# Last recurrence of a two-layer block: the bonus on GpSimd, the first state columns on ScalarE

## The reference

```python
def step(s, rkvw):                      # h = 32 heads, i and j = 16 channels of a head
    r_t, k_t, v_t, w_t = rkvw
    a = k_t[..., :, None] * v_t[..., None, :]
    out = jnp.einsum('bhi,bhij->bhj', r_t, u * a + s)
    s = a + w_t[..., :, None] * s
    return (s, out)
_, out = jax.lax.scan(step, s0, rkvw)   # over the 112 tokens
```

## Time and profile before

| | |
|---|---|
| Median of 3 runs | 1780.87 us (1780.46 to 1786.08) |
| Profiled execution, its own time | 1791.03 us |
| Span of that execution | 1789.2 us |
| TensorE busy, share of the span | 1697.5 us, 95% |
| VectorE busy | 1167.6 us, 65% |
| ScalarE busy | 657.2 us, 37% |
| GpSimd busy | 281.2 us, 16% |
| Mean granted TensorE clock | 0.97 |

### The profile page before, as it was taken

How to read it: one execution, slowest core, us unless ns; L and a number is a source line. 1 busy time by engine, 2 the same in 40 slices (tenths; PEclk the granted TensorE clock), 3 DMA queues, 4 the chain that set the end, 5 groups by cost and what they waited for, 6 DMA issues and landing times.

```text
span 1789.2 us, 18450 instructions
## 1 busy us (share of the span) xinstructions
PE 1697.5 (95%) x6792; PEld 860.0 (48%) x6792; DVE 1167.6 (65%) x1620; ACT 657.2 (37%) x1507; POOL 281.2 (16%) x377
## 2 busy tenths in 40 slices
PE   6999999899999999999999999999989999999968
PEld 3555544345555444445555444455544445444423
DVE  1233200336999895548997965389989767999841
ACT  2466420124666222236663213256532135313111
POOL 1100000122121001121220002211200023136020
PEclk9999999889999999989999999999999999999989
DMA  7001012124111123351120232520022415232131
GB/s 254 12 29 52 1 52 90 50 83 141 37 45 54 41 93 127 97 159 37 37 62 22 88 114 89 157 78 9 16 76 78 135 52 159 85 118 74 56 101 44
DMA packets 75143, 138.82 MB, mean 78 GB/s; under 512 B 16624, under 2 KB 26736, under 8 KB 75056
## 3 DMA queue, kind: packets, MB, share of 16 engines
q1 hardware_dynamic: 60064, 102.36, 17.8%
q0 software_dynamic: 11776, 31.70, 6.0%
q10 hardware_dynamic: 3216, 3.60, 0.7%
HBM read 113.78 MB, written 23.86 MB: 77 GB/s over the span
## 4 chain that ended last, share of the span: by engine, by line
PE 82%; DVE 11%; issue 3%; ACT 3%; ACTq 1%; POOL 0%; DVEq 0%; POOLq 0%
PE bank L324 55%; PE bank L511 12%; PE bank L366 4%; PE bank L358 3%; PE bank L596 3%; DVE C L1315 2%; PE bank L378 2%; DVE sm L1252 1%; PE bank L631 1%; PE bank L346 1%; DVE C L1323 1%; DVE YB L1332 1%; PE bank L610 1%; DVE C L1307 1%; ACT XA L988 1%
## 5 line engine op out<-in xcount | busy, mean ns | idle before, releaser
L1315 DVE TENSOR_TENSOR_SCAN C<-XA,C 128x896 f32<-128x896 f32 x112 | 228.8, 2043 | 3.2
L511 PE MATMUL bank<-ring,HT 128*112 128x512 f32 x512 | 222.3, 592 | 0.0
L1252 DVE CUSTOM_DVE_ANT_0 sm<-bank,maskb 112x375 f32<-112x375 f32 x256 | 124.4, 542 | 139.0 <-PE bank L358 138.5
L324 PE MATMUL bank<-ctx_t,Wk 128*128 128x375 f32 x512 | 200.1, 517 | 14.3 <-DMA Wk<-in_wk 11.3
L324 PE MATMUL bank<-C,ring 128*128 128x448 f32 x512 | 209.2, 565 | 1.4 <-ACT Wk L988 1.4
L324 PE MATMUL bank<-SX,ring 128*128 128x448 f32 (+2 forms) x544 | 195.9, 519 | 4.1 <-issue 4.1
L324 PE MATMUL bank<-Wv,ctx_t 128*125 128x512 f32 x384 | 180.9, 596 | 0.4 <-ACT C L988 0.4
L366 PEld LDWEIGHTS bank<-ident,sm 112*125 112x125 f32 x768 | 124.8, 191 | 106.5 <-ACT sm L1003 44.1
L1009 ACT ACTIVATE probT<-bank 125x336 f32<-125x336 f32 x256 | 114.1, 446 | 164.3 <-PE bank L366 162.7
L1003 ACT ACTIVATE sm<-sm,nm 112x375 f32<-112x375 f32 x256 | 153.4, 599 | 3.3 <-DVE nm L1252 3.1
L511 PEld LDWEIGHTS bank<-ring,HT 128*112 128x112 f32 x512 | 90.6, 177 | 127.2 <-issue 127.2
(11 more groups left out here) (166 smaller groups left out, 2156.3 us busy)
## 6 DMA issues: line engine op xcount, KB each, us to landing
ring<-in_stream SPq DMA_DIRECT2D x64, 1024.0 KB, 5.2
ctx_t<-in_ctxT SPq DMA_DIRECT2D x16, 750.0 KB, 4.7
rkw_scratch<-HT POOLq DMA_DIRECT2D x48, 224.0 KB, 3.1
rkw<-rkw_scratch POOLq DMA_DIRECT2D x24, 224.0 KB, 3.2
HT<-in_x SPq DMA_DIRECT2D x16, 224.0 KB, 5.5
X<-in_x SPq DMA_DIRECT2D x16, 224.0 KB, 5.1
v_scratch<-HT POOLq DMA_DIRECT2D x16, 224.0 KB, 2.7
VB<-v_scratch SPq DMA_DIRECT2D x4, 896.0 KB, 4.5
```

Source lines behind the costliest of these rows:

```text
L324: last_ = nc.tensor.matmul(out_ap, pairs[k][0], pairs[k][1], start=(k == 0), stop=(k == len(pairs) - 1))
L511: last_ = nc.tensor.matmul(bank[SC[b]][0:LQ, :], HT[:, c, b * LQ:(b + 1) * LQ], w[:, c, :], start=(m == 0 and c == 0), stop=(m == 3 and c ...
L1252: nc.vector.tensor_tensor_reduce(out=sm[0:LQ, slot, :], in0=tile(name)[0:LQ, 0:LK], in1=maskb[:, n % 2, :], scale=-SCALE, scalar=3.0e38, o ...
L1315: own.step(nc.vector.tensor_tensor_scan(out=part, data0=wrep[:, i % 2, :], data1=part, initial=0.0, op0=ALU.mult, op1=ALU.add))
```

## The change

In the last recurrence alone, three operations of each of the 16 steps leave VectorE.

- The copy of the first state column (L1310) becomes `first_state(i)` on ScalarE. VectorE waits for `s_first` >= i + 1 before the step's scans. ScalarE does `first_state(0)` and `first_state(1)` at the head of its loop over the steps, and `first_state(i + 1)` in iteration i, behind the decays. What VectorE waited for before it wrote a buffer, ScalarE waits for as well.
- The two bonus operations (L1320 and L1329) become `bonus(i)` on GpSimd: a product r * k, a product with the column of u, and a sum into `bon[:, 0, :]`, each waiting for the one before it. `bonus(i)` stands in iteration i ahead of the load of that iteration and behind `last_add`, `last_std` and `last_store`.
- `load_block` of the last recurrence also waits for `bon_step`, and `group_norm(3)` waits for `bon_step` >= 16.

```diff
@@ -259,6 +259,8 @@
         rkw_in = [sem("rkw_in0"), sem("rkw_in1")]
         wrep_ready = sem("wrep_ready")
         scan_step = sem("scan_step")
+        s_first = sem("s_first")
+        bon_made, bon_step = sem("bon_made"), sem("bon_step")
         summed = sem("summed")
         dve_chain = sem("dve_chain")
         y_norm = sem("y_norm")
@@ -838,11 +840,31 @@
 
             def load_block(p, k):
                 pool.wait_ge(scan_step, p * RS + (k - 1) * BLOCK)
+                if p == NG - 1:
+                    pool.wait_ge(bon_step, (k - 1) * BLOCK)
                 rows = rkw_d[p * P:(p + 1) * P, k * BLOCK:(k + 1) * BLOCK, :, :]
                 to = rkw[:, k % 2, :, :, :]
                 pool.dma_start(to[:, :, 0:2, :].rearrange("p q s t -> p q (s t)"),
                                rows[:, :, 0:2, :].rearrange("p q s t -> p q (s t)")).then_inc(rkw_in[k % 2], 16)
                 pool.dma_start(to[:, :, 2, 1:LQ], rows[:, :, 2, 0:LQ - 1]).then_inc(rkw_in[k % 2], 16)
+
+            def bonus(i):
+
+                blk = rkw[:, (i // BLOCK) % 2, i % BLOCK, :, :]
+                p = NG - 1
+                pool.wait_ge(rkw_in[(i // BLOCK) % 2], 32 * (p * (RS // BLOCK // 2) + i // BLOCK // 2 + 1))
+                if i % BLOCK == 0 and i < 2 * BLOCK:
+                    pool.wait_ge(r_in[i // BLOCK], 16 * NG)
+                if i == 0:
+                    pool.wait_ge(y_norm, p)
+                else:
+                    pool.wait_ge(bon_step, i)
+                nc.gpsimd.tensor_tensor(bon[:, 1, :], blk[:, 0, :], blk[:, 1, :], ALU.mult).then_inc(bon_made, 1)
+                pool.wait_ge(bon_made, 2 * i + 1)
+                nc.gpsimd.tensor_scalar(bon[:, 1, :], bon[:, 1, :], ucol[:, i:i + 1], None, ALU.mult
+                                        ).then_inc(bon_made, 1)
+                pool.wait_ge(bon_made, 2 * i + 2)
+                nc.gpsimd.tensor_tensor(bon[:, 0, :], bon[:, 0, :], bon[:, 1, :], ALU.add).then_inc(bon_step, 1)
 
             def load_first(p, which, done):
 
@@ -906,6 +928,7 @@
                         elif i == 15:
                             last_add(1)
                             last_store(1)
+                        bonus(i)
                         blocks_after(p, i * UNITS, (i + 1) * UNITS)
                     last_add(2)
                     last_store(2)
@@ -1023,6 +1046,23 @@
                                      rkw[:, (i // BLOCK) % 2, i % BLOCK, 2, :].unsqueeze(1).to_broadcast([P, JH, LQ]),
                                      ACT.Copy).then_inc(wrep_ready, 1)
 
+            def first_state(i):
+
+                p = NG - 1
+                if i == 0:
+                    act.wait_ge(s0_in, 64 * NG)
+                    act.wait_ge(mix_ready, 9 * NG)
+                elif i == 1:
+                    ready(act, ("P", p, 3, E - 1))
+                elif i == 2:
+                    ready(act, ("P", p, 4, E - 1))
+                elif i == 3:
+                    for e in range(E):
+                        act.wait_ge(e_out[e], 64 * NG)
+                else:
+                    act.wait_ge(summed, i - 3)
+                nc.scalar.activation(S_last[i % 4][:, :, 0], s0[:, i, :], ACT.Copy).then_inc(s_first, 1)
+
             def decays_after(p, lo, hi):
                 for i in range(2, RS):
                     if lo <= (i - 2) * UNITS + UNITS - 1 < hi:
@@ -1198,8 +1238,13 @@
                     pre(g)
                 else:
                     for i in range(RS):
+                        if i == 0:
+                            first_state(0)
+                            first_state(1)
                         if i > 0:
                             decays_after(p, (i - 1) * UNITS, i * UNITS)
+                            if i + 1 < RS:
+                                first_state(i + 1)
                         if i in (2, 3):
                             last_keys(0, 2 * (i - 2), 2 * (i - 2) + 2)
                         elif i in (4, 5):
@@ -1307,9 +1352,12 @@
                     own.step(nc.vector.tensor_tensor(S[:, :, 1:LQ], VB[:, :, 0:LQ - 1],
                                                      kk[:, 0:LQ - 1].unsqueeze(1).to_broadcast([P, RS, LQ - 1]),
                                                      ALU.mult))
-                    own.step(nc.vector.tensor_copy(S[:, :, 0], s0[:, i, :]))
+                    if not last:
+                        own.step(nc.vector.tensor_copy(S[:, :, 0], s0[:, i, :]))
                 if stage in (1, 2):
                     own.settle()
+                    if last:
+                        dve.wait_ge(s_first, i + 1)
                     dve.wait_ge(wrep_ready, p * RS + i + 1)
                     part = S[:, (stage - 1) * JH:stage * JH, :].rearrange("p j t -> p (j t)")
                     own.step(nc.vector.tensor_tensor_scan(out=part, data0=wrep[:, i % 2, :], data1=part,
@@ -1317,8 +1365,9 @@
                 elif stage == 3:
                     if i % BLOCK == 0 and i < 2 * BLOCK:
                         dve.wait_ge(r_in[i // BLOCK], 16 * (p + 1))
-                    own.step(nc.vector.scalar_tensor_tensor(out=bon[:, 1, :], in0=r, scalar=ucol[:, i:i + 1],
-                                                            in1=kk, op0=ALU.mult, op1=ALU.mult))
+                    if not last:
+                        own.step(nc.vector.scalar_tensor_tensor(out=bon[:, 1, :], in0=r, scalar=ucol[:, i:i + 1],
+                                                                in1=kk, op0=ALU.mult, op1=ALU.mult))
                     own.settle()
                     prod = nc.vector.tensor_tensor(S[:, :, :], S[:, :, :], r.unsqueeze(1).to_broadcast([P, RS, LQ]),
                                                    ALU.mult)
@@ -1326,7 +1375,8 @@
                         prod.then_inc(scan_step, 1)
                     else:
                         own.step(prod)
-                    own.step(nc.vector.tensor_tensor(bon[:, 0, :], bon[:, 0, :], bon[:, 1, :], ALU.add))
+                    if not last:
+                        own.step(nc.vector.tensor_tensor(bon[:, 0, :], bon[:, 0, :], bon[:, 1, :], ALU.add))
                 elif stage == 4 and not last:
                     own.settle()
                     nc.vector.tensor_tensor(YB[:, :, :], YB[:, :, :], S[:, :, :], ALU.add).then_inc(scan_step, 1)
@@ -1337,6 +1387,8 @@
             def group_norm(p):
                 last = p == NG - 1
                 dve.wait_ge(scan_step, p * RS + RS)
+                if last:
+                    dve.wait_ge(bon_step, RS)
                 own.settle()
                 own.step(nc.vector.tensor_tensor(VB[:, :, :], VB[:, :, :], over_j(bon[:, 0, :]), ALU.mult))
                 own.settle()
```

## The result

The changed kernel took 1799.62 us in the median of 5 runs (1790.96 to 1804.39) against 1780.87 (1778.77 to 1786.82). The ratio is 1.0092 (1.0056 to 1.0127): slower, and clear of the noise. A second series of 12 runs gave 1.0051 (1.0027 to 1.0074). Single executions of one kernel lie up to 26 us apart here. The profiled execution shows why a better measure is needed: 1790.96 us, a span of 1789.2 like that of the kernel before, although that one was a long execution and this one a short one. So I measure the stretch from the first product of step 0 to the end of the span. It was 1789.2 - 1511.7 = 277.5 us before, and is 1789.2 - 1501.7 = 287.5 us now: +10.0, forecast +11.3. A second profile of the changed kernel gave 288.4, so differences of under 1 us between two such stretches tell nothing.

The account below looks back on a forecast made before the run. VectorE's queue from 1511.7 to 1656.94, without slack, was taken to set the time. Start loss 11.8, less savings 6.5, plus GpSimd's hold 6.0, gave +11.3 us on 1780.9: 1792 us, range 1784 to 1801.

Parts of the forecast that it names:

- The start: Scans of step 0 wait for first_state(0) behind ScalarE's last Silu; 11.8 us lost by step 2.
- TensorE's own lateness: TensorE waits for the first product with r until 1538.9, but is less late than VectorE, so bounds nothing.
- The savings: Three operations off VectorE save 0.50 us a step, 6.5 us over steps 2 to 14; the added wait is free.
- The port: GpSimd's bonus operations hold VectorE up by turn-taking, by elements: 0.53 us a step, 6.0 us in all.
- GpSimd's queue: Bonuses keep pace; load_block(3, 7) is issued near 1647 and lands near 1650, before step 14 at 1653.5.
- Both have some 3 us to spare: no cost: Block 7's load before step 14, and last_cols(2) before last_mixes(2), each end some 3 us before need.
- if step 14 waits for its load: Sign that the prediction is wrong: VectorE's step 14 has to wait for load_block(3, 7).
- Moved, not saved: last_add(1) leaves steps 13 and 14 and holds up last_mixes(2) instead, 4.2 us in all, ahead of the same products.
- Small operations are free: Rival: 112-element GpSimd operations hold VectorE up as little as one-element ones; +5.3 us, 1786 us; chance 0.13.
- Whole operations: Rival: each bonus operation costs VectorE its whole duration, 1.24 us a step; +20 us, 1801 us; chance 0.10.
- GpSimd too late: Rival: contended GpSimd operations take 0.3 us more each, load of block 7 lands too late; +15, 1796 us; chance 0.09.
- Cover: Rival: the stall at the start has unseen cover, leaving only savings and port; 1780 us; chance 0.04.

Follow-up runs that it names:

- e1: Changed kernel with the bonus back on VectorE, so only the first-column copies go to ScalarE; stretch 288.5 us, ratio to before 1.0053.
- e3: Changed kernel with first_state(0) and first_state(1) moved ahead of the last Silus in ScalarE's queue; stretch 275.6 us, ratio to before 1.0015.
- e5: e3 with bonus(i) and the waits for it left out, so the output lacks that term; stretch 274.8 us, one execution.
- e2: Changed kernel with the first-column copies back on VectorE, so only the bonus goes to GpSimd; stretch 275.6 us, ratio to before 0.9985.
- e4: e3 with GpSimd's last_add(1) behind bonus 15 and three quarters of last_std(2) behind block 7's load; stretch 271.0 us, ratio to before 0.9961.
- e7: e3 with each bonus's r * k product four times as wide, 448 elements in place of 112; stretch 285.6 us, one execution.
- e8: e4 with last_add(1) held back until the last product with r, step 15; stretch 271.5 us, ratio to before 0.9946.

## Why the prediction was right, and where it was not

**The time.** The forecast was 1792 us, from 1784 to 1801. The first median, 1799.62, lies near the upper end, and 18.8 us above the kernel before, of which the stretch explains 10.0. For the mechanism the stretch is the better judge, +10.0 for +11.3.

**The start: right.** 11.8 us were forecast between step 0 and step 2, and 11.75 measured (29.07 - 17.32). e1 shows that this alone makes the loss, e3 that the place in ScalarE's queue makes it. The copy took 0.22 us, not 0.32. TensorE's own lateness bound nothing, as said.

**The savings: right.** A step without bonus takes 8.10 (step 12) and, in e5, 8.11: 0.50 less than 8.60. The additional wait instruction cost nothing that shows.

**The port: right in kind, too high by up to half.** Forecast 0.53 a step, measured 8.35 - 8.10 = 0.25 (steps 2 to 5), in e3 0.34, and in e2, where the copies are still on VectorE, the whole 0.41 that the bonus saves. The term that was mis-sized is the hold of an operation of 112 elements. The changed profile shows how: where VectorE's next instruction follows without a gap, a bonus product costs the full 0.22 that I had worked out (2.22 in place of 2.00 at 1555.81). Where the next instruction waits for the one before (a scan behind a product, a product behind a scan), it costs 0.04 to 0.16, or nothing, in these steps. That VectorE's own gap hides the rest is argued from these rows, not tested by itself.

**GpSimd's queue: wrong by 5.7 us.** "Both have some 3 us to spare: no cost" is the step that failed, and "if step 14 waits for its load" was one of my own signs of being wrong. The load of block 7 was issued 137.6 us after step 0 (1639.34), where I had 135.3 (1647 - 1511.7), and landed 4.7 us later, where I had 3: 4.0 us late in all. VectorE was ready for step 14 at 140.1 us, 1.7 earlier than forecast. So step 14 waited 2.15 us where 3.5 were to be spare, `last_norm(2)` and with it `last_cols(2)` came late as well, and `last_mixes(2)` waited another 0.95. The two errors were of opposite sign: 6.0 us had been allowed for the port, and the port with the waits came to 10.0 - 11.75 + 6.5 = 4.8. The waits are 3.1 of it, so 1.7 is left for the bonus and for `last_add(1)` in its new place. That the sum came out so near was luck in these two terms.

**Moved, not saved: right.** `last_add(1)` ran beside `last_mixes(2)`. From the start of `last_mixes(2)` to ("fk", 2, ..) it was 2.2 us before and is 6.3 now, 0.95 of it the wait. So 3.1 of the forecast 4.2 us fall ahead of those products, and 0.6 between them and step 15. e4 shows what its place is worth.

**The rivals.** "Small operations are free" fell with e7 and with the 0.25. "Whole operations", the rule of the Trainium skill (SBUF — State Buffer, "Who interferes with whom"), gave 1.24 a step and is out by the same number, though the first median lay near its 1801 us. That the two engines take turns is borne out, and for the wide product of e7 (0.94 to 1.17 us lost for 1.14) the rule comes near. "GpSimd too late" came true in its mechanism, with 3.1 us in place of 4. "Cover" for the stall was not there.

## What to carry to other kernels

Before an operation is moved to an engine that has time to spare, look at what stands ahead of it in that engine's queue at the moment it is first needed: a copy of 0.22 us behind a Silu that waited for TensorE cost 12 us, and ahead of that Silu it cost nothing. An engine with a low busy share may still be the wrong one for small operations: three of them, 1.4 us when alone, took about 6 us of GpSimd's queue, which made its loads late. When a bound engine gets faster, ask which engine comes next: here TensorE set the place of step 8, and steps that were 0.33 us faster only made VectorE's waits for it longer, 3.1 us in place of 1.4. And when a new order wins, try it on the old kernel too; that was not done here.

## What the hardware did that I had not expected

When GpSimd's additions began shortly after a product of VectorE, they did not take turns with it. In e3 the product of step 8 took 6.97 us in place of 2.00, first row, while the four additions ran through in 4.92, second row:

```profile
1590.22 6.97 DVE L1351 TENSOR_TENSOR SX<-VB,rkw 128x1776 f32<-128x1776 f32 x1
```

```profile
1590.39 4.92 POOL L820 TENSOR_TENSOR X<-X,ctx_t 112x512 f32<-112x512 f32 x4
```

They began 0.17 us after the product. In the kernel before the first began 0.43 after it (the product of step 8 started at 1583.03), waited for it, and then the engines alternated. The cost to VectorE was 4.97 in the one case and 3.94 in the other. The thirteen traces fall in the same two groups. The additions run through in e3, e4, e5 and e8, where they begin 0.04 to 0.18 us after the product, and they take turns in the other nine, where they begin 0.43 to 1.00 after it. The wide product of e7 that began 0.15 us after a scan (1532.92) also ran through, in 1.14 us, and the scan lost 1.17. What decides who goes first was not tried.
